# Local attention layer: the rotation sums on GpSimd move from the even step into the odd step before it

## The chip, the cores and the metric

The kernel runs on one core of one Trainium2 chip. The metric is the time of the device in microseconds (us). A step of the text below is a step of the kernel's software pipeline, not of the clock.

## The reference

The reference is a stack of four blocks of attention and feed-forward parts over x of 4 × 512 × 128 (the same 2048 rows of 128 are seen as 2 × 1024 rows here). The change touches one part, two layers of local attention with rotary positions. Cut to it:

```
q, k, v = split(shift_token(x) @ wqkv)          # 8 heads of 64
q = q / |q| * q_scale ;  k = k / |k| * k_scale
q = q*cos*scale + rotate_half(q)*sin*scale       # k: divided by scale
k = k*cos/scale + rotate_half(k)*sin/scale
sim  = (8*q) @ k over windows of 64, looking one window back, masked
attn = softmax(sim);  out = attn @ v;  x = x + out @ wo
```

## The kernel before

`local_layer` (line 2235) is called once for each of the two layers. It works on NT = 16 tiles of 128 rows (two batches of eight). The work is a software pipeline written out by hand: all engines walk through the same list of steps n = -4 to 36, and each engine has its own program for a step, in a fixed order; semaphores tie them together. A tile q takes two steps, an even and an odd one. `tile_of(n) = n // 2 + 2` is the tile whose q and k are projected in step n, while scores, exponentials and outputs are those of earlier tiles. Step n's scores are those of four heads (a half) of tile n // 2.

The way of a tile's q and k: TensorE projects them in the even step (`project_qk`), ScalarE squares them (`square`). VectorE multiplies by the cosines in the even step (`cosines`, line 2566) and by the sines at the head of the odd step (`sines`, line 2571). At the end of the odd step it adds up squares per head (`sums`, line 2585) and clamps them (lines 2588 and 2590). GpSimd adds the two products (line 2661, once for q and once for k; for tile 0 VectorE does it), raises the sums to the power -1/2 (line 2664) and multiplies k by it (line 2668). TensorE transposes q and k of the tile in the odd step that follows (`turn_qk`, line 2360), and ScalarE copies them out (line 2486).

The way of the scores: TensorE computes them (lines 2375 and 2380), VectorE takes row maxima (line 2596) and multiplies them by the norms (line 2602, "negated maxima"), ScalarE takes exponentials (line 2510), VectorE inverts the row sums (line 2608), and GpSimd scales the probabilities (`scale_probs`, line 2674). TensorE transposes these (line 2389) two steps after GpSimd scaled them, VectorE copies them out (line 2615), and TensorE multiplies by v (lines 2402, 2409) and by wo (line 2421). In every step TensorE's scores wait until the exponentials of the step before are done.

In an odd step VectorE's order is: sines, maxima and negated maxima of n, reciprocal of n-1, copies, sums and clamps. In an even step: maxima and negated maxima, copies, reciprocal, addition into x, cosines. GpSimd had in an even step the rotation sums, power and product of tile_of(n)-1, then the scaling of step n-1; in an odd step only the scaling of step n-1. The rotated tiles lie in three buffers, the products of cosines and sines in two.

Of the kernel before, what the change touches and what calls it, by code (L numbers as in the profile page):

```python
# [19 lines left out]
ALU = mybir.AluOpType  # L20
# [6 lines left out]
NT = TOKENS // P  # L27
# [2207 lines left out]
def local_layer(nc, m, w, l, Z, tables, qT, kT, v, bands):  # L2235
# [4 lines left out]
    with Phase(nc, f"loc{l}") as ph:  # L2240
# [6 lines left out]
        cospart = m.Y[:].rearrange("p (a k t) n -> p a k (t n)", a=2, k=2)  # L2247
        sinpart = m.HT[:].rearrange("p (a k n) -> p a k n", a=2, k=2)
        rotated = ph.sb("rotated", [P, 3, 2, BANK])
# [26 lines left out]
        def tile_of(n):  # L2276
            return n // 2 + LEAD
# [18 lines left out]
        def turn_at(*unit):  # L2296
            return TURNS.index(unit)
# [355 lines left out]
        @block.gpsimd  # L2653
        def _(pool):
            def rotate(q):
                pool.wait_ge(cs_done, 3 * q + 3)
                if q >= 3:
                    pool.wait_ge(turn_done, turn_at("Q", q - 3, 1) + 1)
                if q >= 1:
                    for k, added in enumerate((addq_done, addk_done)):  # L2660
                        nc.gpsimd.tensor_tensor(rotated[:, q % 3, k, :], cospart[:, q % 2, k, :], sinpart[:, q % 2, k, :],
                                                ALU.add).then_inc(added, 1)
                pool.wait_ge(clamp_done, 2 * q + 2)
                nc.gpsimd.tensor_tensor(norms[:, q, :], sumsq[:, q % 2, :], m.neghalf[:], ALU.pow).then_inc(norm_done, 1)
                pool.wait_ge(addk_done, q + 1)
                pool.wait_ge(norm_done, q + 1)
                kr = rotated[:, q % 3, 1, :].rearrange("p (h d) -> p h d", d=64)
                nc.gpsimd.tensor_tensor(kr, kr, norms[:, q, 8:16].unsqueeze(2).broadcast_to([P, 8, 64]),
                                        ALU.mult).then_inc(kn_done, 1)

            def scale_probs(n):
                pool.wait_ge(rinv_done, n + 1)
                four = probs[:, n % 4, :, :].rearrange("p c (j k) -> p (c j) k", j=2)
                nc.gpsimd.tensor_tensor(four, four, rowsum[:, n % 4, :].unsqueeze(2).broadcast_to([P, 4, SPAN]),
                                        ALU.mult).then_inc(probs_done, 1)

            for n in STEPS:
                q = tile_of(n)
                if n % 2 == 0:
                    if 0 <= q - 1 < NT:  # L2680
                        rotate(q - 1)
                    if 0 <= n - 1 < N:
                        scale_probs(n - 1)
                else:
                    if 0 <= n - 1 < N:
                        scale_probs(n - 1)

# [1404 lines left out]
```

## Time and profile before

| | us |
|---|---|
| three runs, median (lowest to highest) | 3038.31 (3035.02 to 3039.17) |
| the profiled execution | 3042.01 |
| its span, first to last instruction | 3039.1 |
| TensorE matmul busy | 2661.6 |
| VectorE busy | 2059.7 |
| ScalarE busy | 1572.2 |
| GpSimd busy | 1183.1 |
| the scaling of probabilities (line 2674), 64 times | 93.9 |
| the power (line 2664), 32 times | 93.0 |
| the rotation sums (line 2661), 60 times | 74.8 |

The mean granted clock of TensorE is 0.945 of its full speed. The first pass of the local layer fills about 1693 to 1902 us of the span, the second about 1964 to 2173. Busy times of engines overlap, so they don't add up to the span.

### The profile page before, as it was taken

The numbers are of one execution on the slowest core, as the hardware profiler recorded it, in microseconds if no ns is written. First come the engines' busy times: TensorE is split into PE (matmuls) and PEld (weight loads), VectorE is DVE, ScalarE is ACT, GpSimd is POOL, SyncE is SP. The second block draws the span as 40 slices with busy tenths as digits, with TensorE's granted clock in tenths as the row PEclk, the third lists the DMA queues.
The fourth block names the chain that finished last, engine by engine and source line by source line (L and its number), as shares of the span: only waits on it lengthen the run. The fifth ranks groups of instructions, "written<-read, shape, count | busy, mean of one in ns | idle before, by whom it ended". The sixth has DMA issues, their size and how long they took to land. (4 is left out here: it accounts for less than half of the span.)

```text
span 3039.1 us, 55311 instructions
## 1 busy us (share of the span) xinstructions
PE 2661.6 (88%) x21236; PEld 1669.9 (55%) x21236; DVE 2059.7 (68%) x4305; ACT 1572.2 (52%) x3042; POOL 1183.1 (39%) x843
## 2 busy tenths in 40 slices
PE   8985999989799799999999799789777898877898
PEld 5552555566676466566657566456543344334665
DVE  5778999936644655546664576467548999997654
ACT  4444888852433444444554465266457667643422
POOL 3211000001243344434443576177326778773400
PEclk9985999989899899999999899899999999999899
DMA  1000000002120200000000000000013344431000
GB/s 56 1 4 1 3 3 3 3 2 84 34 90 22 86 1 1 1 1 1 1 1 1 29 1 1 1 1 1 1 45 132 134 140 147 144 138 56 1 1 14
DMA packets 34229, 105.41 MB, mean 35 GB/s; under 512 B 3457, under 2 KB 14593, under 8 KB 33201
## 3 DMA queue, kind: packets, MB, share of 16 engines
q1 hardware_dynamic: 31952, 97.69, 9.2%
q0 software_dynamic: 2016, 4.19, 0.4%
q8 instruction: 171, 2.80, 0.4%
q14 instruction: 90, 0.73, 0.1%
HBM read 94.01 MB, written 7.86 MB: 34 GB/s over the span
## 5 line engine op out<-in xcount | busy, mean ns | idle before, releaser
L2159 POOL TENSOR_TENSOR many_probs<-many_probs,many_rinv 128x2048 f32<-128x2048 f32 (+7 forms) x128 | 269.6, 2106 | 358.5 <-DVE many_rinv L2199 358.5
L1139 DVE TENSOR_REDUCE heads_halfmax<-heads_qmajor 128x1 f32<-128x512 f32 x512 | 316.3, 681 | 32.6 <-PE heads_qmajor L1000 29.2
L3638 DVE TENSOR_TENSOR_SCAN stream_state<-stream_decay,stream_state 128x512 f32<-128x512 f32 x256 | 306.3, 1233 | 0.5
L1104 ACT ACTIVATE weights<-heads_kmajor 128x1024 f32<-128x1024 f32 x256 | 259.2, 1026 | 71.5 <-PE heads_kmajor L1012 65.7
L2128 ACT ACTIVATE many_probs<-many_score,many_negmax 128x1024 f32<-128x1024 f32 (+7 forms) x256 | 187.4, 737 | 173.1 <-DVE many_negmax L2183 173.1
L2183 DVE TENSOR_REDUCE many_negmax<-many_score 128x1 f32<-128x1024 f32 (+7 forms) x256 | 184.4, 751 | 106.0 <-PE many_score L2057 104.4
L3308 PE MATMUL stream_yacc<-stream_state,ident 128*128 128x512 f32 x512 | 249.0, 614 | 0.4 <-POOL stream_state L3600 0.4
L3600 POOL TENSOR_TENSOR stream_state<-XN,stream_state 128x1024 f32<-128x1024 f32 x85 | 200.2, 2358 | 79.9 <-DVE stream_state L3638 79.6
L3470 ACT ACTIVATE stream_decay<-weights,mamba_negA 128x512 f32<-128x512 f32 x256 | 173.0, 689 | 112.1 <-DVE stream_state L3638 110.8
L2065 PE MATMUL many_ring<-ident,many_probs 128*128 128x128 f32 x1152 | 174.6, 279 | 23.4 <-POOL many_probs L2159 6.5
L2510 ACT ACTIVATE loc_probs<-loc_score,loc_negmax,loc_norms 128x192 f32<-128x192 f32 x256 | 127.3, 507 | 119.9 <-DVE loc_negmax L2602 119.9
L3629 DVE TENSOR_TENSOR stream_state<-stream_bspread,stream_du 128x1024 f32<-128x1024 f32 x128 | 153.2, 1197 | 45.3 <-POOL stream_du L3576 38.8
L2118 ACT ACTIVATE many_probsT<-many_ring 128x512 f32<-128x512 f32 x192 | 107.7, 561 | 137.3 <-PE many_ring L2065 137.2
L1028 PE MATMUL heads_outp<-weights,heads_vaug 128*9 128x128 f32 x4096 | 161.0, 276 | 13.5 <-ACT heads_outT L1097 13.2
L2065 PEld LDWEIGHTS many_ring<-ident,many_probs 128*128 128x128 f32 x1152 | 125.1, 140 | 86.1 <-DVE many_zT L2193 32.7
L2081 PE MATMUL many_ring<-many_probsT,many_v 128*64 128x128 f32 x2304 | 153.8, 278 | 12.5 <-ACT many_probsT L2118 12.4
L2053 PE MATMUL many_score<-many_kT,many_qT 64*128 64x512 f32 (+3 forms) x768 | 158.6, 517 | 1.2 <-ACT many_probs L2128 1.2
L3308 PEld LDWEIGHTS stream_yacc<-stream_state,ident 128*128 128x128 f32 x512 | 101.4, 198 | 90.2 <-issue 72.1
L3299 PE MATMUL stream_bspread<-stream_BC,stream_select 128*128 128x512 bf16 x256 | 81.3, 401 | 77.6 <-DVE stream_state L3629 70.9
L2081 PEld LDWEIGHTS many_ring<-many_probsT,many_v 128*64 128x64 f32 x2304 | 123.2, 136 | 32.3 <-ACT many_probsT L2118 20.3
L2596 DVE TENSOR_REDUCE loc_rowmax<-loc_score 128x4 f32<-128x768 f32 x64 | 61.3, 957 | 115.7 <-PE loc_score L2380 115.7
L1160 POOL CAST heads_qstack<-heads_negmax 128x16 bf16<-128x16 f32 x16 | 4.1, 256 | 338.0 <-DVE heads_negmax L1129 338.0
(598 smaller groups left out, 6156.2 us busy)
## 6 DMA issues: line engine op xcount, KB each, us to landing
XN<-mamba_crows SPq DMA_DIRECT2D x85, 512.0 KB, 3.6
stream_crow<-mamba_crows SPq DMA_DIRECT2D x43, 512.0 KB, 3.6
weights<-in_w_dram SPq DMA_DIRECT2D x1, 6148.0 KB, 17.3
weights<-in_w_dram SPq DMA_DIRECT2D x1, 4274.0 KB, 14.4
weights<-in_w_dram SPq DMA_DIRECT2D x1, 3296.0 KB, 10.5
swiglu_pairs<-swiglu_fetched SPq DMA_DIRECT2D x1, 2310.0 KB, 10.4
weights<-in_w_dram SPq DMA_DIRECT2D x1, 2112.0 KB, 7.9
swiglu_fetched<-swiglu_pairs SPq DMA_DIRECT2D x4, 528.0 KB, 6.4
```

Source lines behind the costliest of these rows:

```text
L1028: last = nc.tensor.matmul(outp[32 * j:32 * j + 9, 0, c * P:(c + 1) * P], vaug[:, b * TPB + kc, 4 * c + j, :], probs_of(4 * q + j // 2 * 2 ...
L1104: nc.scalar.activation(probs_of(k).rearrange("p (a n) -> p a n", a=2), kmajor[:, at:at + 2, :], ACT.Exp, scale=SC).then_inc(exp_done, 1)
L1139: nc.vector.tensor_reduce(halfmax[:, g % 2, at, h % 2:h % 2 + 1], qmajor[:, (2 * n + j) % 3, :], AX, ALU.max).then_inc(max_done, 1)
L2065: last = nc.tensor.transpose(ring[:, k % 2, x % 4 * P:(x % 4 + 1) * P], probs[:, n % 4, x * P:(x + 1) * P], m.ident[:])
L2081: last = nc.tensor.matmul(ring[DH * h:DH * (h + 1), k % 2, 0:P], v[:, g % 2, kb, DH * h:DH * (h + 1)], probsT[:, n % 2, x * P:(x + 1) * P] ...
L2128: nc.scalar.activation(probs[:, n % 4, h * wide:(h + 1) * wide], score_of(n, h)[:, 0:wide], ACT.Exp, bias=negmax[:, n % 3, h:h + 1], accum ...
L2159: nc.gpsimd.tensor_tensor(pair, pair, rinv[:, n % 4, :].unsqueeze(2).broadcast_to([P, 2, wide]), ALU.mult).then_inc(norm_done, 1)
L2183: nc.vector.tensor_reduce(negmax[:, n % 3, h:h + 1], score_of(n, h)[:, 0:(UNITS[n][1] + 1) * P], AX, ALU.max, negate=True).then_inc(negmax ...
L3308: last = nc.tensor.matmul(yacc[:, half, :], m.ident[:], state[:, g % STATES, part(half)], start=(g % NS == 0), stop=(g % NS == NS - 1))
L3470: nc.scalar.activation(decay[:, h % DECAYS, :], delta_of(j, ch)[:, part(half)], ACT.Exp, scale=negA[:, a:a + 1]).then_inc(dec_done, 1)
L3600: nc.gpsimd.tensor_tensor(state[:, g % STATES, :], crow_of(g), state[:, g % STATES, :], ALU.mult).then_inc(hc_done, 1)
L3638: nc.vector.tensor_tensor_scan(h[:, part(half)], decay[:, (2 * g + half) % DECAYS, :], h[:, part(half)], 0.0 if half == 0 else h[:, BANK - ...
```

## The change

GpSimd's function `rotate` is cut in two. `rotate(q)` keeps the waits and the two rotation sums, and `normalise(q)` has power and product. In an odd step GpSimd now makes the rotation sums of tile_of(n) ahead of the scaling of step n-1; in the even step that follows it begins with power and product, and then scales. Tile 0 has its sums made by VectorE, as before, so `rotate` is called for tiles 1 to 15.

```diff
                 pool.wait_ge(cs_done, 3 * q + 3)
                 if q >= 3:
                     pool.wait_ge(turn_done, turn_at("Q", q - 3, 1) + 1)
-                if q >= 1:
-                    for k, added in enumerate((addq_done, addk_done)):
-                        nc.gpsimd.tensor_tensor(rotated[:, q % 3, k, :], cospart[:, q % 2, k, :], sinpart[:, q % 2, k, :],
-                                                ALU.add).then_inc(added, 1)
+                for k, added in enumerate((addq_done, addk_done)):
+                    nc.gpsimd.tensor_tensor(rotated[:, q % 3, k, :], cospart[:, q % 2, k, :], sinpart[:, q % 2, k, :],
+                                            ALU.add).then_inc(added, 1)
+
+            def normalise(q):
                 pool.wait_ge(clamp_done, 2 * q + 2)
                 nc.gpsimd.tensor_tensor(norms[:, q, :], sumsq[:, q % 2, :], m.neghalf[:], ALU.pow).then_inc(norm_done, 1)
                 pool.wait_ge(addk_done, q + 1)
...
                 if n % 2 == 0:
                     if 0 <= q - 1 < NT:
-                        rotate(q - 1)
+                        normalise(q - 1)
                     if 0 <= n - 1 < N:
                         scale_probs(n - 1)
                 else:
+                    if 1 <= q < NT:
+                        rotate(q)
                     if 0 <= n - 1 < N:
                         scale_probs(n - 1)
```

## Rows read from the trace of the kernel before

**Rows 1.** The page, busy time of each engine, share of the span, instructions.
```profile
PE 2661.6 (88%) x21236; PEld 1669.9 (55%) x21236; DVE 2059.7 (68%) x4305; ACT 1572.2 (52%) x3042; POOL 1183.1 (39%) x843
```

**Rows 2.** Window of the first pass: length, busy PE, PEld, DVE, ACT, POOL, PEclk, DMA, GB/s.
```profile
1693.00:1934.00 241.00, 207.73 (x1484) 142.23 (x1485) 153.72 (x326) 128.75 (x375) 149.86 (x98) 0.96 0.00 1
```

**Rows 3.** Waits in first and second pass: total us, times, longest us.
```profile
PE loc_turned L2360 <- POOL loc_rotated L2668: 14.3, 11, 4.6
...
PE loc_turned L2360 <- POOL loc_rotated L2668: 14.7, 12, 4.5
```

**Rows 4.** Timeline of TensorE, first pass: start, duration, [idle before and releaser].
```profile
1722.52 0.82 PE L2360 MATMUL loc_turned<-ident,loc_rotated 128*128 128x128 f32 x4 [3.65 <-POOL loc_rotated L2668]
1723.27 1.65 PE L2375 MATMUL loc_score<-loc_kT,loc_qT 64*128 64x192 f32 x8
...
1735.16 0.63 PE L2360 MATMUL loc_turned<-ident,loc_rotated 128*128 128x128 f32 x4 [2.22 <-POOL loc_rotated L2668]
...
1782.88 0.63 PE L2360 MATMUL loc_turned<-ident,loc_rotated 128*128 128x128 f32 x4 [0.72 <-POOL loc_rotated L2668]
...
1807.29 0.63 PE L2360 MATMUL loc_turned<-ident,loc_rotated 128*128 128x128 f32 x4 [0.28 <-POOL loc_rotated L2668]
...
1864.78 0.92 PE L2375 MATMUL loc_score<-loc_kT,loc_qT 64*128 64x192 f32 x8
...
1875.61 0.63 PE L2360 MATMUL loc_turned<-ident,loc_rotated 128*128 128x128 f32 x4 [1.36 <-POOL loc_rotated L2668]
```

**Rows 5.** Timeline of TensorE, start of the second pass.
```profile
1994.61 1.09 PE L2360 MATMUL loc_turned<-ident,loc_rotated 128*128 128x128 f32 x4 [4.23 <-POOL loc_rotated L2668]
1995.63 1.65 PE L2375 MATMUL loc_score<-loc_kT,loc_qT 64*128 64x192 f32 x8
...
2007.51 0.63 PE L2360 MATMUL loc_turned<-ident,loc_rotated 128*128 128x128 f32 x4 [1.87 <-POOL loc_rotated L2668]
```

**Rows 6.** Windows, two neighbouring periods of the first pass, columns as in rows 2.
```profile
1795.43:1806.35 10.92, 10.92 (x91) 7.70 (x89) 8.84 (x18) 7.29 (x24) 8.30 (x6) 1.00 0.01 2
1806.35:1817.74 11.39, 11.11 (x91) 7.68 (x89) 8.68 (x18) 7.31 (x24) 9.26 (x7) 1.00 0.01 2
```

**Rows 7.** Timeline of TensorE and VectorE over one period.
```profile
1796.45 0.92 PE L2375 MATMUL loc_score<-loc_kT,loc_qT 64*128 64x192 f32 x8
...
1796.37 1.27 DVE L2571 TENSOR_TENSOR HT<-loc_proj,loc_scaled 128x512 f32<-128x512 f32 x2
1797.84 0.96 DVE L2596 TENSOR_REDUCE loc_rowmax<-loc_score 128x4 f32<-128x768 f32 x1 [0.20 <-PE loc_score L2380]
...
1801.15 0.73 DVE L2588 TENSOR_SCALAR loc_sumsq<-loc_sumsq 128x8 f32<-128x8 f32 x1
...
1804.72 0.16 DVE L2602 TENSOR_TENSOR loc_negmax<-loc_rowmax,loc_norms 128x4 f32<-128x4 f32 x1
...
1807.13 1.28 DVE L2571 TENSOR_TENSOR HT<-loc_proj,loc_scaled 128x512 f32<-128x512 f32 x2
```

**Rows 8.** Timeline of GpSimd over the same period.
```profile
1793.06 1.04 POOL L2668 TENSOR_TENSOR loc_rotated<-loc_rotated,loc_norms 128x512 f32<-128x512 f32 x1
...
1799.16 1.47 POOL L2674 TENSOR_TENSOR loc_probs<-loc_probs,loc_rowsum 128x768 f32<-128x768 f32 x1 [2.48 <-DVE loc_rowsum L2608]
1800.59 2.50 POOL L2661 TENSOR_TENSOR loc_rotated<-Y,HT 128x512 f32<-128x512 f32 x2
1803.05 2.91 POOL L2664 TENSOR_TENSOR loc_norms<-loc_sumsq,neghalf 128x16 f32<-128x16 f32 x1
1806.10 1.04 POOL L2668 TENSOR_TENSOR loc_rotated<-loc_rotated,loc_norms 128x512 f32<-128x512 f32 x1
```

**Rows 9.** Timeline of ScalarE: the last of an even step's exponentials.
```profile
1806.80 0.21 ACT L2510 ACTIVATION_READ_ACCUMULATOR loc_probs<-loc_score,loc_negmax,loc_norms 128x1 f32 x1
```

**Rows 10.** Timeline of VectorE: negated maxima of two other even steps.
```profile
1719.46 0.16 DVE L2602 TENSOR_TENSOR loc_negmax<-loc_rowmax,loc_norms 128x4 f32<-128x4 f32 x1
...
1793.81 0.31 DVE L2602 TENSOR_TENSOR loc_negmax<-loc_rowmax,loc_norms 128x4 f32<-128x4 f32 x1
```

## The prediction

> **What bounds the kernel now.** I looked first at how busy the engines are over the whole span: TensorE 2661.6 of 3039.1 us, GpSimd 1183.1 [rows 1]. That says little, because the edit touches only the two passes of the local layer, 1693 to 1934 and 1964 to 2205 us. In the first TensorE is busy 207 of 241 us, VectorE 154, GpSimd 150, ScalarE 129 [rows 2]. The reader should see that TensorE leads, but leaves 33 us in gaps. The view of waits says who makes them: TensorE's transposes of the rotated tile wait for GpSimd's normalised k (line 2668) 14.3 us in the first pass (11 times) and 14.7 us in the second (12 times) [rows 3]. So 29 us is what stands on the edited code.
>
> The single waits have two sizes [rows 4, 5]. At the start of a pass they are 4.6 (4.5 in the second, both from [rows 3]), then 3.65 and 2.22 (second pass 4.23 and 1.87); in the middle 0.28; once 0.72; at the end 1.36. A middle one costs more than it shows. A period is two steps, one 128-row tile. The period from 1795.43 has no wait and takes 10.92 us with TensorE busy throughout; the next has the 0.28 wait and takes 11.39 [rows 6]. The 0.47 between them is the wait and a refill.
>
> Why 11.39? GpSimd runs, one behind another: scaling of probabilities 1.47 (start 1799.16), two rotation sums 2.50, power 2.91 (1803.05), product 1.04 (1806.10, ends 1807.14), and TensorE takes k at 1807.29 [rows 4, 8]. The scaling cannot start before VectorE's reciprocal, which stands behind the odd step's maxima, which stand behind that step's scores, which stand behind the transpose of k. That is a closed ring through the rotation sums, though their input, the sine products, was ready at 1797.64 (1796.37 + 1.27), before the scaling began [rows 7, 8].
>
> **The change, part by part.** No instruction is added or removed: 30 pairs of sums still take 2.5 us each on GpSimd, and its load of 2 × 1.47 + 2.50 + 2.91 + 1.04, with a gap of 0.14, is 9.5 us a period, under TensorE's 10.92. No DMA is issued in these steps (DMA share 0.00, [rows 2]), so no queue is passed.
>
> Call S the start of the odd step's scores, 1796.45 [rows 7]. The offsets today: row maxima S+1.39, negated maxima about S+2.38 (0.99 after), first clamp S+4.70, the even step's negated maxima S+8.27, its exponentials' end S+10.56 (1806.80 + 0.21), the next sine products' end S+11.96, which is 1.04 after the next free S at S+10.92 [rows 6 to 9].
>
> New order: the sums start at about S+1.14, end at S+3.6; the scaling that stood ahead of them now runs from about S+3.65 to S+5.1. The added wait (for the sine products, ahead of the scaling) can hold only the scaling; its reader is TensorE's transpose of probabilities a whole period later, so I cost that at nothing; without that cover it would be 0.5 us. The clamp (S+4.70) meets the scaling on GpSimd and, I take it, ends at S+5.3. Power then runs from S+5.45, product from S+8.5 to S+9.55, k can be taken at S+9.7. TensorE reaches k at S+10.92−1.02+0.55 = S+10.45 by itself. The wait goes, and what is late next is TensorE's own work: 10.92.
>
> *A shared port, and where it could hurt.* The clamp took 0.73 us at 1801.15 and ended as the first of the two sums did (1800.59 + 1.25); the negated maxima took 0.31 instead of 0.16 when they met the product (1793.06 to 1794.10) and ended with it; against a running power they took 0.16 [rows 7, 8, 10]. So these small VectorE operations wait out the sums, scalings and products, but not the power. The moved sums now lie beside the odd step's negated maxima: first sum S+1.14 to S+2.4, negated maxima at S+2.38. They meet the seam and lose 0 to 0.1; bounds 0 and 1.25 (a whole second sum). Even 1.25 costs TensorE under 0.1: negated maxima to the last exponential is 2.29 (S+8.27 to S+10.56), so the odd ones end at S+4.67, and the even scores start 1.39 before their maxima (S+8.27 less 0.99), at S+5.89. In the even step the negated maxima (S+8.27) now pass just ahead of the product (S+8.5): 0; bounds 0 and 1.04. There the exponentials have only 10.92−10.56 = 0.36 of slack, so a full meeting would cost TensorE 0.7. I take 0, since the clamp is held until the scaling ends, which puts the product behind; the margin is 0.2 us.
>
> The Trainium skill, page "SBUF — State Buffer", section "Who interferes with whom", says that a VectorE instruction with two SBUF inputs contends with a GpSimd instruction that reads SBUF, and that whoever issues first makes the other wait in full. That speaks against this change and fits the rows for sums and product. Taken for every GpSimd instruction it would also have held today's 1804.72 until the power ended at 1805.96, and the row shows 0.16; by the row I leave the power out.
>
> *Sum, middle.* Small waits: six in the first pass, seven in the second, 13 × 0.47 = 6.1. The 0.72 wait with its 0.19 refill, twice: 1.8.
>
> *End of a pass.* The last k is taken at 1875.61, with S at 1864.78 with the k before it: S+10.83 [rows 4]. New: S+9.7. Twice 1.15 = 2.3.
>
> *Start of a pass.* The 4.6 stays: it is the first tile's power, whose sums VectorE makes, as before. Next wait (3.65, 4.23): the scaling is now followed by the power at once, not by 2.46 of sums. Against that, about 0.35 of clamp is exposed and up to 0.3 of meeting sums at the negated maxima: k comes 1.9 earlier. In the second pass I take all of it. In the first, the product would start at about 1719.40, the negated maxima at 1719.46 [rows 10]: I let them collide, exponentials then end at about 22.8 and scores start there instead of at 1723.27 [rows 4]: gain 0.5 (bounds 0.5 and 1.5). Third wait (2.22, 1.87): scores ran at half speed, S to k took 11.89 and 11.88 [rows 4, 5]. The sums leave the chain (2.46), but now the clamp ends later than the scaling starts by about 1.0, so 1.4 remains in each. Start: 0.5 + 1.4 + 1.9 + 1.4 = 5.2.
>
> Total 6.1 + 1.8 + 2.3 + 5.2 = 15.4 us. The profiled execution took 3042.0 (span 3039.1), so it would be 3026.6; it lies 3.7 above the median of the three runs, 3038.3, and against that the forecast is **3023 us**.
>
> Bounds: if all waits on GpSimd but the two first (29.0 − 9.1) went, with 0.19 refill on 21 of them, 24 us are gained: 3014. Clock: the granted clock is 0.96 of full in these stretches [rows 2], and the 1.65 us scores against 0.92 [rows 4, 5, 7] show the slow level after the long start waits. Shorter waits might avoid some of it, up to about 2 us a pass, or leave it; I take nothing.
>
> **Rivals.**
> (1) *Every second even step collides.* If the product wins the seam, exponentials are held 1.04, TensorE waits 0.7 and that period takes 11.6. By my offsets the sine products then also end later, the clamp slips and the next product starts at about S+8.8, free again. Average 11.3, gain 0.1 instead of 0.47 on 13 periods, and nothing for the 0.72s: 15.4 − 4.8 − 1.8 = 8.8 gained, 3030 (3027 to 3033). For it: the margin is only 0.2. Against: the held clamp restores the free order.
> (2) *The wait only changes its name.* TensorE waits for exponentials as much as it did for k, time 3038. For it: scores already wait for exponentials near the ends of passes. Against: the free period [rows 6] has the same VectorE and ScalarE work and no wait.
> (3) *Slower: the even negated maxima wait behind the product in every period.* Place: line 2602 behind line 2668, decided when the product starts before S+8.27, that is if the clamp isn't held by the scaling. Price: all full periods take 11.6. That is +0.2 on 13 of them and +0.7 on seven that have no wait on k today (32 tiles, less 23 waits, less the two that fill the pipeline): 7.5 us lost. Of the start and end gains, 7.5 in the sum, collisions would leave about 1.5: 3044. By the skill's rule of the port, named above, this is what first-come would give if GpSimd came first; the rows show both orders possible.
> (4) *More than forecast*, the slow clock at the starts avoided: 3019; inside my own range.
>
> **Chances.** Forecast (3018 to 3027) 0.60; more than that 0.05; rival (1) 0.17; rival (2) 0.11; rival (3) 0.07. Range with 8 in 10: 3015 to 3034, its ends from the 24 us bound and from rival (1) with 4 us of scatter (the three runs span 4.2). 0.2% is 6 us, about what a measurement here tells from no change. Faster by more: 0.60 + 0.05 + 0.15 = 0.80; same: 0.14; slower: 0.06.
>
> **What would show it.** In the new profile: (a) the sums start 0.1 us after the sine products, and scaling follows; (b) waits of k on line 2668 fall from 29 us to about 12 (two first ones, remnants at the starts, 0.3 at the ends); (c) middle periods of 10.92; (d) the clamp (2588) meets the scaling, not a sum: about 0.4 to 0.5 instead of 0.73; (e) negated maxima (2602) stay near 0.16 in even steps, lengthen slightly in odd ones. I am wrong if line 2602 shows 0.5 to 1.2 us in even steps and TensorE's scores wait for line 2510 by as much.

## The result, and the profile after

The changed kernel took 3031.29 us (median of 7 runs, 3024.34 to 3035.98), the kernel before 3039.17 (7 runs, 3035.02 to 3042.61). The ratio is 0.9963, 95% interval 0.9952 to 0.9974. By the ratio that is 11.2 us faster, between 7.9 and 14.6; the two medians lie 7.9 apart. Forecast was 15.4 less, 3023. The profiled execution took 3033.28, span 3031.2.

First the windows of the changed kernel, in the columns of [rows 2]. The first is the middle period that answers to [rows 6]; then the period at the seam between the two batches (in short, the batch seam) in the first and in the second pass; then the period ahead of the last k, in both passes.

```profile
1795.45:1806.37 10.92, 10.92 (x91) 7.70 (x89) 9.22 (x18) 7.20 (x24) 8.71 (x6) 1.00 0.01 2
1779.93:1795.45 15.52, 13.22 (x95) 9.33 (x93) 9.22 (x18) 8.03 (x25) 9.79 (x8) 0.89 0.00 1
2046.27:2060.38 14.11, 11.82 (x94) 8.46 (x93) 9.22 (x18) 7.92 (x25) 9.78 (x8) 1.00 0.01 2
1860.96:1873.51 12.55, 10.25 (x85) 8.06 (x83) 9.09 (x17) 6.66 (x24) 10.97 (x8) 0.86 0.00 1
2125.92:2136.84 10.92, 8.63 (x85) 6.67 (x83) 8.96 (x17) 6.00 (x22) 9.34 (x7) 1.00 0.01 2
```

The middle is what was forecast: 10.92 us with TensorE busy throughout, against 11.39 [rows 6]. But VectorE is busy 9.22 us of it where it was 8.68 to 8.84, though it does the same work. The period at the batch seam took 13.93 us before, and takes 14.11 or 15.52 now. The two passes of the same code differ by 1.4 us there, and the granted clock is 1.00 in one and 0.89 in the other.

The view of waits, first pass (total us, times, longest), against [rows 3]:

```profile
PE loc_score L2375 <- ACT loc_probs L2510: 8.1, 6, 2.4
...
PE loc_turned L2360 <- POOL loc_rotated L2669: 6.4, 2, 4.5
...
PE loc_shared L2349 <- issue: 2.3, 1, 2.3
```

The wait for k has gone from 14.3 us in 11 pieces to 6.4 in 2; over both passes it is 12.8. What has grown is in TensorE's timeline: the projection of v at the batch seam waits 2.30 us, as do the scores before the last k.

```profile
1787.30 1.19 PE L2349 MATMUL loc_shared<-weights,loc_HS 128*128 128x256 f32 x2 [2.30 <-issue]
...
1867.89 0.97 PE L2375 MATMUL loc_score<-loc_kT,loc_qT 64*128 64x192 f32 x8 [2.30 <-ACT loc_probs L2510]
...
2053.63 0.67 PE L2349 MATMUL loc_shared<-weights,loc_HS 128*128 128x256 f32 x2 [2.29 <-issue]
```

Both waited 1.20 us in the kernel before:

```profile
1788.68 0.67 PE L2349 MATMUL loc_shared<-weights,loc_HS 128*128 128x256 f32 x2 [1.20 <-issue]
...
1869.59 0.92 PE L2375 MATMUL loc_score<-loc_kT,loc_qT 64*128 64x192 f32 x8 [1.20 <-ACT loc_probs L2510]
```

The first row after the change runs its two matmuls in 1.19 us, the third in 0.67: after the same wait TensorE was at the slow level once and at full speed once. What holds them is in the timelines of GpSimd and VectorE over one middle period, to be laid beside [rows 7, 8]. The second row is the second of the two sums in the first row, as a later window shows it by itself:

```profile
1797.59 2.49 POOL L2660 TENSOR_TENSOR loc_rotated<-Y,HT 128x512 f32<-128x512 f32 x2 [1.04 <-DVE HT L2571]
1798.82 1.27 POOL L2660 TENSOR_TENSOR loc_rotated<-Y,HT 128x512 f32<-128x512 f32 x1
1800.27 1.47 POOL L2675 TENSOR_TENSOR loc_probs<-loc_probs,loc_rowsum 128x768 f32<-128x768 f32 x1 [0.18 <-DVE loc_rowsum L2608]
...
1797.86 0.96 DVE L2596 TENSOR_REDUCE loc_rowmax<-loc_score 128x4 f32<-128x768 f32 x1 [0.35 <-PE loc_score L2380]
1798.85 1.25 DVE L2602 TENSOR_TENSOR loc_negmax<-loc_rowmax,loc_norms 128x4 f32<-128x4 f32 x1
```

The negated maxima start at 1798.85, 0.03 us after the second sum (1798.82), and take 1.25 us instead of 0.16. They end at 1800.10, as the second sum does (1800.09). They wait out the whole second sum, in ten odd steps of this pass. Their reader, the exponentials, starts 1.1 us later. In the middle this is hidden: the last exponential ends at 1802.22 (1802.02 + 0.20), and the scores that wait for it start at 1802.36 without a wait.

```profile
1802.02 0.20 ACT L2510 ACTIVATION_READ_ACCUMULATOR loc_probs<-loc_score,loc_negmax,loc_norms 128x1 f32 x1
...
1802.36 0.92 PE L2375 MATMUL loc_score<-loc_kT,loc_qT 64*128 64x192 f32 x8
```

At the batch seam ScalarE must copy v behind these exponentials before TensorE can project the next v:

```profile
1783.34 1.25 DVE L2602 TENSOR_TENSOR loc_negmax<-loc_rowmax,loc_norms 128x4 f32<-128x4 f32 x1
...
1786.50 0.21 ACT L2510 ACTIVATION_READ_ACCUMULATOR loc_probs<-loc_score,loc_negmax,loc_norms 128x1 f32 x1
1786.60 0.60 ACT L2494 ACTIVATE loc_v<-loc_shared 128x512 f32<-128x512 f32 x1
```

The copy ends at 1787.20, and the projection of v starts at 1787.30. Ahead of the last k there is no projection of q and k to fill the time. At these two places the 1.1 us is TensorE's loss, twice a pass.

### The profile page after: what moved, and what is told of

It is laid out like the page before. It is cut to its first block and busy times, and to the rows that moved or that the text cites. A ratio compares the mean times of both kernels' runs of the same rounds, so it can differ in the third digit from the quotient of the medians.

```text
span 3031.2 us, 55309 instructions
## 1 busy us (share of the span) xinstructions
PE 2661.3 (88%) x21236; PEld 1670.4 (55%) x21236; DVE 2068.6 (68%) x4305; ACT 1571.0 (52%) x3042; POOL 1186.3 (39%) x843
## 5 line engine op out<-in xcount | busy, mean ns | idle before, releaser
L1028 PE MATMUL heads_outp<-weights,heads_vaug 128*9 128x128 f32 x4096 | 162.1, 277 | 13.5 <-ACT heads_outT L1097 13.2
L2081 PE MATMUL many_ring<-many_probsT,many_v 128*64 128x128 f32 x2304 | 153.8, 278 | 12.5 <-ACT many_probsT L2118 12.4
L225 POOL TENSOR_TENSOR norm_rstd<-norm_rstd,neghalf 128x4 f32<-128x4 f32 x46 | 46.8, 1017 | 219.0 <-DVE norm_rstd L219 219.0
```

The lines of the kernel that those rows point to most:

```text
L1028: last = nc.tensor.matmul(outp[32 * j:32 * j + 9, 0, c * P:(c + 1) * P], vaug[:, b * TPB + kc, 4 * c + j, :], probs_of(4 * q + j // 2 * 2 ...
L2081: last = nc.tensor.matmul(ring[DH * h:DH * (h + 1), k % 2, 0:P], v[:, g % 2, kb, DH * h:DH * (h + 1)], probsT[:, n % 2, x * P:(x + 1) * P] ...
```

## The experiments

Each kernel was timed beside the kernel before on the same chip. The medians compare best among kernels that were timed together: e1 to e4 (kernel before 3040.48), e5 to e8 (3042.07), e9 and e10 (3043.61). Of e1 to e3 only e2 has an interval that lies clear of the changed kernel's (e4, 0.9956 to 0.9979); for the others the traces carry the argument.

**e1: scaling between the sums.**

```diff
-                for k, added in enumerate((addq_done, addk_done)):
-                    nc.gpsimd.tensor_tensor(rotated[:, q % 3, k, :], cospart[:, q % 2, k, :], sinpart[:, q % 2, k, :],
-                                            ALU.add).then_inc(added, 1)
+                nc.gpsimd.tensor_tensor(rotated[:, q % 3, k, :], cospart[:, q % 2, k, :], sinpart[:, q % 2, k, :],
+                                        ALU.add).then_inc((addq_done, addk_done)[k], 1)
...
                     if 1 <= q < NT:
-                        rotate(q)
+                        rotate(q, 0)
                     if 0 <= n - 1 < N:
                         scale_probs(n - 1)
+                    if 1 <= q < NT:
+                        rotate(q, 1)
```

> Odd step on GpSimd: sum of q, scaling, sum of k (the changed kernel: both sums, then scaling). Port theory: the shortfall of the change comes from the odd step's negated maxima (2602) waiting out the second sum, 1.25 us. Here the scaling follows the first sum, and it waits for a reciprocal that stands behind the negated maxima, so nothing is running when they come: 2602 0.16 to 0.3 in odd steps; TensorE's longest waits at the batch seam and before the last tile 1.2 instead of 2.3 us; no slow clock there; middle periods stay 10.92. Time 3 to 6 us under the changed kernel, 3025 to 3028. Rival (TensorE only came earlier to a place that something else bounds): these waits stay at 2.3 and the time is the changed kernel's within 1 us.

Measured: 3025.10 us, ratio 0.9951 (0.9937 to 0.9966). Timelines of VectorE and GpSimd in a middle period:

```profile
1792.68 1.27 POOL L2659 TENSOR_TENSOR loc_rotated<-Y,HT 128x512 f32<-128x512 f32 x1 [1.03 <-DVE HT L2571]
1794.27 1.47 POOL L2674 TENSOR_TENSOR loc_probs<-loc_probs,loc_rowsum 128x768 f32<-128x768 f32 x1 [0.32 <-DVE loc_rowsum L2608]
...
1793.95 0.16 DVE L2602 TENSOR_TENSOR loc_negmax<-loc_rowmax,loc_norms 128x4 f32<-128x4 f32 x1
```

The negated maxima come at the same place, as the first sum ends (1793.95), find nothing running, and take 0.16. The wait at the batch seam is 1.20 in both passes, the period there 13.02. Part of the gain is given back at the start, where the second sum is behind the scaling again: k is awaited 3.00 and 2.59 us instead of 1.84 and 1.94, and the passes take 198.69 and 197.44. In one even step of each pass the negated maxima start 0.03 us after the product and wait it out (1.03 us); the period there takes 11.12 where it took 10.57 in the changed kernel.

**e2: the second sum waits for the negated maxima.**

```diff
-            def rotate(q):
+            def rotate(q, n):
...
                 for k, added in enumerate((addq_done, addk_done)):
+                    if k == 1 and 0 <= n < N:
+                        pool.wait_ge(negmax_done, n + 1)
                     nc.gpsimd.tensor_tensor(rotated[:, q % 3, k, :], cospart[:, q % 2, k, :], sinpart[:, q % 2, k, :],
                                             ALU.add).then_inc(added, 1)
```

> The changed kernel, but the sum of k waits until the negated maxima of that odd step are done. Port theory: 2602 ends with the first sum (0.16 to 0.2 us), the second sum starts about 0.2 late, waits of 2.3 fall to 1.2, middle periods 10.92, time 3025 to 3028. Rival (bounded by something else): waits stay 2.3, the time is the changed kernel's.

Measured: 3022.97 us, ratio 0.9939 (0.9924 to 0.9953). It is 2 us less than expected. Waits at the batch seam 1.21 and 1.20, middle periods 10.92, negated maxima 0.16 in the odd steps. Adding a wait to GpSimd made the kernel 7 us faster than the changed one timed with it (3030.40). That refutes, for these places, the rival that TensorE merely arrived earlier somewhere bounded by another thing.

**e3: a memset ahead of the sums.**

```diff
+        unread = ph.sb("unread", [P, 128])
...
+                nc.gpsimd.memset(unread[:], 0.0)
                 for k, added in enumerate((addq_done, addk_done)):
```

> The changed kernel with one more GpSimd instruction, a memset of 128x128 ahead of the two sums, about 0.2 us, which puts the sums later. Port theory, with the seam between the sums open to who has waited long enough: negated maxima now come some 0.2 us before the seam and get in there, 2602 0.3 us in odd steps instead of 1.25, and more work on GpSimd makes the kernel 2 to 5 us faster than the changed one. Rival (GpSimd keeps the port from sum to sum): 2602 about 1.45 us in odd steps, time equal to the changed kernel or up to 2 us slower.

Measured: 3025.44 us, ratio 0.9951 (0.9933 to 0.9970). A middle period, the second sum again by itself as well:

```profile
1802.97 0.20 POOL L2660 MEMSET loc_unread<- 128x128 f32 x1 [1.01 <-DVE HT L2572]
1803.13 2.50 POOL L2662 TENSOR_TENSOR loc_rotated<-Y,HT 128x512 f32<-128x512 f32 x2
1804.36 1.27 POOL L2662 TENSOR_TENSOR loc_rotated<-Y,HT 128x512 f32<-128x512 f32 x1
...
1804.25 0.17 DVE L2603 TENSOR_TENSOR loc_negmax<-loc_rowmax,loc_norms 128x4 f32<-128x4 f32 x1
```

The sums start 0.16 us later. The negated maxima now start 0.11 before the second sum (1804.36), get in between the two sums and are done at 1804.42. The batch seam costs 1.22 us of wait again, the period there 13.04, the passes 196.44 and 196.41 us against 200.62 and 197.46 of the changed kernel. My price for the passage, 0.3, was too high; the direction was right.

**e4: the changed kernel once more.** Same code, for a second trace.

> The changed kernel once more on this chip, for a second trace. Middle periods 10.92 and 2602 at 1.25 in odd steps again in both passes; which of the four waits of 2.3 us are followed by slow clock may differ from the first trace (there two, both in the first pass); time 3027 to 3034, 0.2 to 0.5% under the kernel before.

Measured: 3030.40 us, ratio 0.9968 (0.9956 to 0.9979), 12 runs. All four long waits are 2.29 again. Its passes took 199.53 and 197.40; the period before the last k took 12.51 in the first pass (granted clock 0.86) and 10.91 in the second (1.00), so one slow stretch lay there, and none at the batch seam (14.12, 1.00).

**e5: the same memset in the kernel before.**

```diff
+        unread = ph.sb("unread", [P, 128])
...
                 if q >= 1:
+                    nc.gpsimd.memset(unread[:], 0.0)
                     for k, added in enumerate((addq_done, addk_done)):
```

> The kernel before (sums in the even step, behind the scaling) with the same memset of 128x128 ahead of the two sums as in e3. Ring theory: here the memset (0.16 us from its start to the sum's) lies in the ring scaling, sums, power, product, transposes, scores, maxima, reciprocal, so the middle periods grow from 11.39 to 11.55 and every start wait by 0.16: 2 to 5 us slower than the kernel before, where in e3 the same instruction gained 5. Rival (GpSimd's load or the spacing of port users sets the pace, not the ring): no slower than the kernel before, or faster as in e3.

Measured: 3049.44 us, ratio 1.0017 (1.0004 to 1.0029): slower. TensorE's timeline, q and k in two middle periods:

```profile
1815.74 0.63 PE L2361 MATMUL loc_turned<-ident,loc_rotated 128*128 128x128 f32 x4 [0.43 <-POOL loc_rotated L2670]
...
1827.27 0.63 PE L2361 MATMUL loc_turned<-ident,loc_rotated 128*128 128x128 f32 x4 [0.43 <-POOL loc_rotated L2670]
```

The period is 11.53 (1827.27 − 1815.74), 0.14 to 0.15 more than 11.39 [rows 6], about what the memset puts ahead of the sums. The same instruction that gained 5 us by the medians in the new order costs 5 (1 to 9, from the ratio) in the old. So the sums stood in a closed ring in the old order, and stand outside it in the new. One part of the expectation missed: not every start wait grew. The second did (4.38 in both passes, against 3.65 and 4.23), the third shrank (1.86 and 1.45, against 2.22 and 1.87).

**e6: a memset of 16 columns.**

```diff
-        unread = ph.sb("unread", [P, 128])
+        unread = ph.sb("unread", [P, 16])
```

> The changed kernel with a memset of only 128x16 ahead of the sums, about 0.07 us, so that the odd step's negated maxima come less than 0.1 us before the seam between the sums. If the seam is open to whoever already waits: 2602 0.16 to 0.25 us in odd steps and time as e3, 3023 to 3027. If it takes a longer wait to be let in: 2602 about 1.3 us, and the time is the changed kernel's, 3028 to 3032.

Measured: 3022.47 us, ratio 0.9932 (0.9916 to 0.9949). A middle period, in the same way:

```profile
1800.26 0.11 POOL L2660 MEMSET loc_unread<- 128x16 f32 x1 [1.02 <-DVE HT L2572]
1800.32 2.51 POOL L2662 TENSOR_TENSOR loc_rotated<-Y,HT 128x512 f32<-128x512 f32 x2
1801.55 1.28 POOL L2662 TENSOR_TENSOR loc_rotated<-Y,HT 128x512 f32<-128x512 f32 x1
...
1801.53 0.16 DVE L2603 TENSOR_TENSOR loc_negmax<-loc_rowmax,loc_norms 128x4 f32<-128x4 f32 x1
```

The first sum starts 0.06 us after the memset does. That puts the second sum at 1801.55, 0.02 after the negated maxima, and they pass. In the changed kernel it started 0.03 ahead of them. A few hundredths of a microsecond decide over 1.1. One odd step near the start of the first pass still took 1.11; there the second sum had started first.

**e7 and e8: the power left out,** in the old and in the new order. The norms are the constant 0.25, so q and k are not normalised; all waits stay.

```diff
-                nc.gpsimd.tensor_tensor(norms[:, q, :], sumsq[:, q % 2, :], m.neghalf[:], ALU.pow).then_inc(norm_done, 1)
+                nc.gpsimd.tensor_tensor(norms[:, q, :], m.neghalf[:], m.neghalf[:], ALU.mult).then_inc(norm_done, 1)
```

> The kernel before with the norms made as a constant (neghalf times neghalf, 0.25) in place of the power: the l2 normalisation is left out, every wait is kept. 2.9 us become about 0.1. Ring theory: the ring falls from 11.39 to about 8.6, under TensorE's 10.92, so middle periods are 10.92 although the sums stand behind the scaling; start waits shrink by 2.5 or more each. 2602 stays 0.16. Time 3015 to 3022. Rival (the old place of the sums costs by itself): middle periods stay over 11.

> The changed kernel with the power left out in the same way (norms are the constant 0.25). Ring and port theory together: the ring is gone either way, so the new order has nothing left to gain and keeps its price: 2602 at 1.25 us in odd steps, two waits of 2.3 us a pass. So it is 2 to 6 us slower than e7. Rival (the new order is better by itself): it is as fast as e7 or faster.

Measured: e7 3019.47 us, ratio 0.9920 (0.9902 to 0.9938); e8 3023.90, ratio 0.9941 (0.9922 to 0.9960). The transposes of q and k in the middle of e7's first pass, and VectorE's negated maxima in e8:

```profile
1801.10 1.09 PE L2360 MATMUL loc_turned<-ident,loc_rotated 128*128 128x128 f32 x8
...
1812.01 1.09 PE L2360 MATMUL loc_turned<-ident,loc_rotated 128*128 128x128 f32 x8
```

```profile
1796.67 1.25 DVE L2602 TENSOR_TENSOR loc_negmax<-loc_rowmax,loc_norms 128x4 f32<-128x4 f32 x1
```

In e7 the period is 10.91 with the sums in their old place: shorten the ring by other means and the reordering has nothing to gain. e8 keeps the price, 1.25 in the odd step and waits of 2.29 at the batch seam. It is 4.4 us slower than e7; the intervals overlap, but the passes agree: 194.3 and 194.2 us against 191.3 and 193.6.

**e9 and e10: the small memset and the changed kernel again, side by side.** e9 is e6's kernel, e10 the changed one.

> e6's kernel (changed kernel, memset of 128x16 ahead of the sums) on another occasion with five rounds, beside the changed kernel on the same chip. Port theory: 3022 to 3026, 4 to 8 us under the changed kernel, passes of 196 to 197 us; every odd step's 2602 under 0.3 in the middle. Rival (its e6 time was scatter of four runs): within 2 us of the changed kernel.

> The changed kernel, as comparison for e9 on the same chip: 3028 to 3033, 0.3 to 0.4% under the kernel before; passes 197.4 us where the two waits of 2.3 us are followed by full clock, 1 to 3 us longer where they aren't.

Measured: e9 3022.10 us, ratio 0.9937 (0.9919 to 0.9955); e10 3026.98, ratio 0.9951 (0.9935 to 0.9968). The time of e10 is 1 us below what was expected. The passes of e9 took 196.22 and 196.23, those of e10 199.90 and 197.45. By medians e9 is 4.9 us faster; the two intervals overlap, so from the times alone a gain over the changed kernel is likely and not shown. In the passes of the traces it is plain: six passes of the changed kernel took 197.40 to 200.62 us, six with a memset (e3, e6, e9) 196.16 to 196.44.

## Why the prediction was right, and where it was short

I compare by passes, from the first transposes of q to the first matmul of the part that follows. Before, each took 205.29 us; after, 200.62 and 197.46: 12.5 us gained. The rest of the two profiled executions differs by 4.6 the other way, in code that the edit doesn't touch. With the traces of e4 and e10 (199.53 + 197.40 and 199.90 + 197.45) the gain in the passes is 12.5, 13.7 and 13.2, against 15.4 forecast and 11.2 (7.9 to 14.6) measured in the times.

| us gained, both passes | forecast | measured |
|---|---|---|
| start | 5.2 | 9.0 |
| middle | 5.2 | 5.2 |
| batch seam | 1.8 | −1.8 |
| tail | 3.2 | 0.2 |
| sum | 15.4 | 12.6 |

In the table two of the thirteen small waits are counted with the tail, where they lie. The ring was right. The batch seam and the tail came out 6.6 us short by a collision that I had priced at next to nothing: about 3.6 by the wait itself, 3.0 by the slow clock that followed it in the first pass. The start gained 3.8 more than I had reckoned. That these errors had opposite signs is luck. The time, 3031.29, is inside my range of 3015 to 3034, but above the 3018 to 3027 to which I gave 0.60; it falls into the 3027 to 3033 of rival (1), whose mechanism is not what made it.

*Ring and middle, right.* Forecast 13 × 0.47 = 6.1. Ten of the thirteen lay in full periods of 11.38 to 11.40, now 10.91 to 10.94, and one in a period of 11.89 that is now 11.40: 5.2. The other two lay in the periods before the last k, which the tail's sum below includes. e5 and e7 show the ring itself: longer by 0.15 when it gets 0.16 of work, gone when the power is out.

*Start, undersized.* Forecast 5.2, of which 1.9 (0.5 + 1.4) in the first pass and 3.3 (1.9 + 1.4) in the second; the first four periods gained 4.65 and 4.30, 9.0 in sum. The third wait, which I let shrink by 1.4, went altogether in both passes. Two errors went the same way. I let the negated maxima of the first pass collide with the product. They did not: 1722.34 against 1722.40, the 0.06 us that I had seen and read as a collision.

```profile
1722.34 0.16 DVE L2602 TENSOR_TENSOR loc_negmax<-loc_rowmax,loc_norms 128x4 f32<-128x4 f32 x1
...
1722.40 1.04 POOL L2669 TENSOR_TENSOR loc_rotated<-loc_rotated,loc_norms 128x512 f32<-128x512 f32 x1
```

And I took nothing for the clock. The start's second half (third and fourth period) had a granted clock of 0.88 before, in the window 1718.27 to 1747.23, and has 0.93 now:

```profile
1721.15:1745.63 24.48, 21.63 (x145) 14.81 (x144) 18.60 (x37) 15.23 (x49) 20.56 (x14) 0.93 0.01 1
```

The same stretch in the kernel before:

```profile
1718.27:1747.23 28.96, 23.09 (x146) 15.81 (x144) 18.62 (x37) 15.65 (x49) 22.83 (x16) 0.88 0.00 1
```

The surplus of the second pass, 1.0, owes nothing to the collision, which I had assumed in the first alone. How the 2.8 of the first pass split I have not separated.

*Batch seam, the step that failed.* Of the odd step's negated maxima I had written (its seam is the one between the two sums): "They meet the seam and lose 0 to 0.1; bounds 0 and 1.25 (a whole second sum). Even 1.25 costs TensorE under 0.1." The upper bound came true in nearly every odd step. Its price was right in the middle (the exponentials end at 1802.22 and the scores start at 1802.36) and wrong at the batch seam, which I had counted at 1.8 gained and never checked for slack. Measured: 15.52 and 14.11 against 13.93, 1.8 lost. With the collision taken away (e1, e2, e3, e6) the period is 13.02 to 13.04, just the 0.9 a pass that I had forecast.

*Tail, the same failure.* From the second-last transposes of q on, the pass took 38.68 us, now 39.40 and 37.76. In e3, without the collision, it is 37.01 and 37.01. The forecast (38.68 less 0.47 and 1.15) was 37.06.

*Rivals.* Rival (1) put the collision into the even step. In each pass one even step took 0.48 or 0.47 us and all others 0.16 or 0.17, so its mechanism hardly occurred. Rival (2) is wrong in the middle and right at two places a pass. Rival (3) did not occur: in every other even step the negated maxima started ahead of the product.

For the middle that was no test of my margin of 0.2. The odd step's wait held up the clamp too: it starts at 1802.26 and takes 0.17, clear of the scaling (ended 1801.74), where I had let it meet the scaling and take 0.4 to 0.5 (sign d). So power and product came later than in my working, and the even step's negated maxima, at 1804.74, were 0.90 ahead of the product (1805.64). The kernels without the odd collision are the test. In their middle periods the negated maxima started ahead of the product by 0.36 (e1), 0.28 (e2), 0.15 (e3) and 0.07 us (e6), and took 0.16 each time, and in e3 and e6 the clamp met the scaling and took 0.51 and 0.43. The product of e6's middle period:

```profile
1807.42 0.16 DVE L2603 TENSOR_TENSOR loc_negmax<-loc_rowmax,loc_norms 128x4 f32<-128x4 f32 x1
...
1807.49 1.04 POOL L2671 TENSOR_TENSOR loc_rotated<-loc_rotated,loc_norms 128x512 f32<-128x512 f32 x1
```

A VectorE instruction of two SBUF inputs waited out a whole GpSimd sum, 1.25 us for 0.16. So says the rule of the Trainium skill that I had set beside the rows, page "SBUF — State Buffer", section "Who interferes with whom": who issues first makes the other wait in full. The trace agrees, down to a few hundredths: in the changed kernel the second sum had started 0.03 us before. I trusted the rule for the even step, and for the odd one I believed in the seam between the sums. That was worth 5 to 7 us by the medians of e1 to e4.

*The slow clock makes the changed kernel's passes differ.* In each of its three traces the clock fell to the slow level after one or both of the first pass's waits of 2.3 us: at the batch seam in the first trace (15.52 against 14.11, 1.4 us, granted clock 0.89) and in e10 (15.75, 1.6 us, 0.89), ahead of the last k in the first trace and in e4 (12.55 and 12.51 against 10.91, 1.6 us, 0.86). In e1, e2, e3, e6 and e9, whose waits there are 1.2, it fell at neither place; but it did not fall at e8's four waits of 2.29 either, and it fell after the next wait of 1.63 us in e9's first pass (scores in 1.30 us instead of 0.92). That the longer wait brings the slow clock is therefore likely and not shown. Nor does this explain the scatter of whole runs: e9's six span 14.6 us, e10's 11.5.

## What to carry to other kernels

When an instruction that moves off a closed ring has to lie somewhere else, list who contends with it there for SBUF, and price each meeting at its upper bound in every kind of period: the first, the last and the odd one out have less slack than the middle. A meeting whose margin is under 0.1 us is not forecast by subtraction; give it both prices. And a doubtful mechanism can be tested by adding work: one small memset gained about 5 us in one order and lost about as much in the other, which no account of loads can explain.

## What the runs showed that I had not expected

- Where two GpSimd sums follow each other, a VectorE instruction with two inputs in SBUF passes or waits by who starts first. In the middle of a pass the records of e6 and e9 have it start 0.01 to 0.03 us before the second sum, those of e3 0.11 to 0.13, and it took 0.16 to 0.19 us. In the changed kernel it started 0.01 to 0.04 us after the second sum, and took 1.24 to 1.27.
- The power (2.91 us, 128x16) let the negated maxima pass in 0.16 to 0.17 us wherever they met, in every trace that has it. Sums and product did not. Scaling held up the clamp (0.64 us in e2 instead of 0.17); the negated maxima never met it.
- The same wait of 2.3 us was followed by slow clock in some passes and not in others, in one execution of one program.
